# Folding a head's two output parts on TensorE with a constant 73x37 matrix, and dividing straight from PSUM

## What is computed

```python
qkv = h @ W_qkv + b_qkv
qkv = qkv.reshape(b, l, 3, H, D)
q, k, v = (qkv[:, :, 0], qkv[:, :, 1], qkv[:, :, 2])
scale = D ** (-0.5)
scores = jnp.einsum('blhd,bmhd->bhlm', q * scale, k)
attn = jax.nn.softmax(scores, axis=-1)
o = jnp.einsum('bhlm,bmhd->blhd', attn, v).reshape(b, l, c)
return o @ W_proj + b_proj
```

## Time and profile before

| | |
|---|---|
| median of 3 runs | 2692.27 us (2688.56 to 2693.1) |
| the profiled execution's own time | 2695.13 us |
| its span, first to last instruction | 2693.5 us |
| attention stage, about | 130 to 1500 us |
| TensorE busy (matmul records) | 2381.8 us, 88% |
| TensorE weight loads | 2048.1 us, 76% |
| VectorE busy | 1433.2 us, 53% |
| ScalarE busy | 1097.7 us, 41% |
| GpSimd busy | 772.7 us, 29% |
| mean granted TensorE clock | 0.939 |

### The profile page before, as it was taken

The page is one execution under the profiler, slowest core; times in us unless marked ns, Lnnn a source line. Parts: engine busy times, 40 slices in busy tenths (PEclk is TensorE's granted clock), DMA queues, the critical chain, the costliest instruction groups (busy, mean ns, idle before and its releaser), DMA issues. The chain is left out here.

```text
span 2693.5 us, 48930 instructions
## 1 busy us (share of the span) xinstructions
PE 2381.8 (88%) x15081; PEld 2048.1 (76%) x15081; DVE 1433.2 (53%) x2978; ACT 1097.7 (41%) x2362; POOL 772.7 (29%) x1547
## 2 busy tenths in 40 slices
PE   5698988988989789798998467999999999999998
PEld 1465766756767567576675457999999999999998
DVE  3577676676776766767766473333333333333332
ACT  1265555555555555555655122222222222222221
POOL 1043343343444344334445481111111111111110
PEclk9799989989989899898998688999999999999998
DMA  7122122231222222212221141010101010110100
GB/s 224 43 75 78 54 80 66 63 96 43 86 72 58 76 67 68 89 54 74 75 66 55 62 122 50 27 43 27 39 27 39 27 38 28 38 36 30 36 25 27
DMA packets 90196, 160.52 MB, mean 60 GB/s; under 512 B 22832, under 2 KB 34176, under 8 KB 89920
## 3 DMA queue, kind: packets, MB, share of 16 engines
q1 hardware_dynamic: 77056, 110.35, 14.2%
q0 software_dynamic: 11856, 46.60, 5.3%
q10 hardware_dynamic: 1024, 0.26, 0.0%
HBM read 80.10 MB, written 20.16 MB: 37 GB/s over the span
## 5 line engine op out<-in xcount | busy, mean ns | idle before, releaser
L1649 PE MATMUL bank<-h2T,w 128*128 128x256 f32 x4032 | 531.1, 283 | 9.3 <-issue 6.5
L1649 PEld LDWEIGHTS bank<-h2T,w 128*128 128x128 f32 x4032 | 508.0, 191 | 10.9 <-issue 7.6
L1558 DVE TENSOR_TENSOR glo<-bank,ghi 128x256 fp32r<-128x256 f32 x288 | 122.3, 425 | 688.2 <-ACT bank L1525 688.2
L1662 PE MATMUL bank<-w,ghi 128*128 128x288 f32 x2304 | 476.5, 298 | 0.4
L1524 ACT ACTIVATE ghi<-bank,b 128x256 fp32r<-128x256 f32 x288 | 137.1, 476 | 687.9 <-PE bank L1649 687.8
L869 DVE TENSOR_TENSOR plo<-pf,phi 128x512 fp32r<-128x512 f32 x512 | 365.3, 713 | 87.5 <-ACT pf L738 82.5
L735 ACT ACTIVATE phi<-bank 128x512 fp32r<-128x512 f32 x512 | 303.1, 592 | 252.0 <-PE bank L1049 226.5
L862 DVE TENSOR_REDUCE negm<-bank 128x1 f32<-128x512 f32 x512 | 349.5, 683 | 101.4 <-PE bank L1021 87.7
L1662 PEld LDWEIGHTS bank<-w,ghi 128*128 128x128 f32 x2304 | 367.2, 189 | 2.5 <-DVE x2T L1568 2.0
L1662 PE MATMUL bank<-w,glo 128*128 128x288 f32 x1152 | 340.8, 296 | 0.0
L738 ACT ACTIVATE pf<-bank 128x512 f32<-128x512 f32 x512 | 303.2, 592 | 0.0
(11 more groups left out here) (222 smaller groups left out, 3226.3 us busy)
## 6 DMA issues: line engine op xcount, KB each, us to landing
xln<-x POOLq DMA_DIRECT2D x16, 1152.0 KB, 6.8
qs<-qkhi SPq DMA_DIRECT2D x192, 72.0 KB
ks<-qkhi SPq DMA_DIRECT2D x192, 72.0 KB
wst<-w_fc POOLq DMA_DIRECT2D x34, 288.0 KB, 3.0
x_d<-xln POOLq DMA_DIRECT2D x32, 288.0 KB, 2.5
xa<-x_d SPq DMA_DIRECT2D x32, 288.0 KB, 2.8
xs<-x_d SPq DMA_DIRECT2D x16, 576.0 KB, 3.8
out<-xs SPq DMA_DIRECT2D x16, 576.0 KB, 2.9
```

What stands on the lines that cost most here:

```text
L1649: mm = pe.matmul(F[ft % 2][:, 0:CH], w1[0:rows, w, ft * PAR:(ft + 1) * PAR], h[0:rows, a, :], start=(i == 0), stop=(i == len(FULL_PASSES) ...
L1662: mm = pe.matmul(Y[2 * tt + half][:, 0:HALF], g[ft % 2][:, span], w2[:, ft, w, half * HALF:(half + 1) * HALF], start=(ft == 0 and i == 0), ...
```

## The change

TensorE no longer transposes `ots`. It multiplies it, as stationary operand, by a constant matrix `fold` of 73x37: the first 36 columns have a one at row j and one at row 37 + j, the last column a one at row 36. So the product is transposed and its parts are added in one step, and 37 columns a piece come out instead of 73. It is a plain fp32 product, as lines 997 and 1007 are. VectorE then takes the reciprocal, and multiplies from PSUM straight into `early` or `oo`; `oraw`, the reduction and GpSimd's `divide` go away. The semaphore `o_read` goes too: `o_norm` is raised by VectorE and takes its place in all waits. The two waits of `divide` (for `early_moved`, and for the last transposed output tile) move to VectorE. GpSimd gets a wait ahead of the second load of x, and `fold` is made by two VectorE instructions at the start of the stage.

```diff
-        oraw = [sb(acts, f"oraw{i}", [PAR, TT, HD]) for i in range(2)]
+        fold = sb(acts, "fold", [2 * HD + 1, HD + 1])
-        OW = 2 * HD + 2
+        OW = HD + 2
-        CONSTANTS = RING + 5
+        CONSTANTS = RING + 7
...
+                    if isinstance(b, int) and b == 1:
+                        pool.wait_ge(g_full, g_use(-1, ("ln", KT)) + 1)
                     load_x(pool, b)
...
-                def divide(b, n):
-
-                    h = (n // TT - 1) % HEADS
-                    pool.wait_ge(o_read, b * HEADS + n // TT + 1)
-                    if h < EARLY:
-                        if h == 0 and (not isinstance(b, int) or b >= 1):
-                            pool.wait_ge(early_moved, b)
-                        head = early[:, :, h * HD:(h + 1) * HD]
-                    else:
-                        if h == EARLY and (not isinstance(b, int) or b >= 1):
-                            pool.wait_ge(g_full, g_use(b, ("tr", TT - 1)) + 1)
-                        head = oo[:, :, h * HD:(h + 1) * HD]
-                    pool.tensor_tensor(head, oraw[h % 2][:, :, :], recip[h % 2][:, :].unsqueeze(2).to_broadcast([PAR, TT, HD]), ALU.mult).then_inc(o_norm, 1)
...
-                    if n % TT == 3 and is_there(b, n - TT):
-                        divide(b, n)
...
+                rows = ident[0:2 * HD + 1, :]
+                dve.tensor_tensor(fold[:, 0:HD], rows[:, 0:HD], rows[:, HD + 1:2 * HD + 1], ALU.add).then_inc(fixed, 1)
+                dve.tensor_copy(fold[:, HD:HD + 1], rows[:, HD:HD + 1]).then_inc(fixed, 1)
...
                     dve.wait_ge(oT, ho + 3)
-                    dve.wait_ge(o_norm, ho + 1)
                     dve.reciprocal(recip[i][:, :], view[:, :, HD]).then_inc(recip_done, 1)
-                    pair = view[:, :, 0:2 * (HD + 1)].rearrange("p t (two d) -> p t d two", two=2)[:, :, 0:HD, :]
+                    h = (n // TT - 1) % HEADS
+                    if h < EARLY:
+                        if h == 0 and (not isinstance(b, int) or b >= 1):
+                            dve.wait_ge(early_moved, b)
+                        head = early[:, :, h * HD:(h + 1) * HD]
+                    else:
+                        if h == EARLY and (not isinstance(b, int) or b >= 1):
+                            dve.wait_ge(g_full, g_use(b, ("tr", TT - 1)) + 1)
+                        head = oo[:, :, h * HD:(h + 1) * HD]
                     dve.wait_ge(recip_done, ho + 1)
-                    dve.tensor_reduce(oraw[i][:, :, :], pair, AX.X, ALU.add).then_inc(o_read, 1)
+                    dve.tensor_tensor(head, view[:, :, 0:HD], recip[i][:, :].unsqueeze(2).to_broadcast([PAR, TT, HD]), ALU.mult).then_inc(o_norm, 1)
...
                     pe.wait_ge(ot_done, ho + 2)
-                    pe.wait_ge(o_read, ho + 1)
+                    pe.wait_ge(o_norm, ho + 2)
...
                     for qt in range(TT):
-                        mm = pe.transpose(X[:, qt * OW:qt * OW + 2 * HD + 1], ots[i][:, qt * PAR:(qt + 1) * PAR],
-                                          ident[0:2 * HD + 1, 0:2 * HD + 1])
+                        mm = pe.matmul(X[:, qt * OW:qt * OW + HD + 1], ots[i][:, qt * PAR:(qt + 1) * PAR], fold[:, :], start=True, stop=True)
                     mm.then_inc(oT, 1)
```

More of the change, by code:

```diff
@@ L455, in build @@
         s_full, exp_f, exp_hi, p_lo, pv = sem("s_full"), sem("exp_f"), sem("exp_hi"), sem("p_lo"), sem("pv")
-        ot_done, oT, recip_done, o_read, o_norm = sem("ot_done"), sem("oT"), sem("recip_done"), sem("o_read"), sem("o_norm")
+        ot_done, oT, recip_done, o_norm = sem("ot_done"), sem("oT"), sem("recip_done"), sem("o_norm")
         early_moved = sem("early_moved")
@@ L553, in _ @@
                 pool.sem_inc(xo_done, 2)
-                pool.sem_inc(o_norm, 2)
                 pool.sem_inc(row_ready, 1)
@@ L799, in _ @@
                 dve.sem_inc(m_read, 2)
-                dve.sem_inc(o_read, 1)
+                dve.sem_inc(o_norm, 2)
                 def modulate(it, f):
@@ L964, in transpose_out @@
                         pe.wait_ge(early_moved, it)
-                    pe.wait_ge(o_read, it * HEADS + (TR_SLOT[qt] // TT + 1 if is_there(it, 0) else 1))
+                    pe.wait_ge(o_norm, it * HEADS + (TR_SLOT[qt] // TT + 2 if is_there(it, 0) else 2))
                     if is_there(it, TR_SLOT[qt] + 5):
@@ L1027, in transpose_max @@
                     if is_there(b, TT * (h - 3)):
-                        pe.wait_ge(o_read, b * HEADS + h - 1)
+                        pe.wait_ge(o_norm, b * HEADS + h)
                     pe.transpose(XM, negm[h % 2][:, :], ident[:, :]).then_inc(mT, 1)
```

## The result

The changed kernel takes 2734.64 us, median of 4 runs (2732.7 to 2737.6); the kernel before took 2692.68 us beside it. The ratio is 1.0155, 95% interval 1.0141 to 1.0169: slower by 42 us. The forecast was 2751, slower by 59 (than the 2692.3 that it started from).

The account below looks back on a forecast made before the run. TensorE's queue bounds the attention stage: 2695.1 + 88 (longer step) - 27 (covered by waits) - 1 (VectorE) - 1 (GpSimd) = 2754, forecast 2751 us since the profiled execution was 2.9 above the median; own range 2735 to 2770, outer 2715 to 2783.

Parts of the forecast that it names:

- What bounds the stage: Attention stage: most slots end when TensorE's queue ends; VectorE and ScalarE have slack and follow it.
- The price of a record: TensorE's new products: eight records a head at 0.111 us, 0.89 us against 0.31 for four transpositions, 0.58 extra.
- Rival 2: TensorE's products cost by the columns they move: at most 26 us extra, more than half covered, about 2702 us; chance 0.08.
- Half clock: Heads where TensorE runs at half clock: 19 of 128, each 1.31 us extra, 24.9 us in all.
- The cover: TensorE's later waits in the same slot, ten of 16 places, absorb 3.65 us an item, 27 us in all.
- My allowance for the first and last items: The first and last batch items cover less, so 3.65 us was multiplied by 7.3 items.
- the others: Slots outside the ten covering, three dense and three next to long gaps: -2 us forecast.
- VectorE, GpSimd: Relief from VectorE's shorter step and GpSimd's missing divide: 1 us credit each, ends 0 to 8 and 0 to 4.
- Rival 1: No cover: the waits behind TensorE's transposition move with it, 2780 us; chance 0.10.
- Rival 4: VectorE sets the slots, so TensorE's addition is free and VectorE's 0.17 us a head counts: 2671 us; chance 0.04.
- Rival 3: TensorE's clock falls less often with matmuls for transpositions; six full items lose 30 us, 2721 us; chance 0.08.
- Its own test: Signs in the trace: records 111 ns apart, step 1.12 us, items near 182 us, line 997's GpSimd waits smaller.

Follow-up runs that it names:

- the transposed kernel: Changed kernel with TensorE's four transpositions of 73 columns a head restored, VectorE still multiplying from PSUM, no GpSimd divide: 2690.44 us, ratio 0.9986 to the kernel before.
- eight heads in waiting slots: Changed kernel with the product only for eight heads an item where TensorE waits behind the step, the others transposed: 2696.05 us, ratio 1.0012 to the kernel before.
- the doubled products: Changed kernel with each of a head's four products issued twice, 16 records instead of 8: 2908.91 us, ratio 1.0811 to the kernel before.
- the filled kernel before: Kernel before with 40 idle transpositions of 128 columns in slot 40's wait for GpSimd, first seven items: 2682.41 us, ratio 0.9962.
- the filled changed kernel: Changed kernel with the same 40 idle transpositions of 128 columns in slot 40: 2724.31 us, ratio 1.0121 to the kernel before.
- plain products: Kernel before with 20 plain fp32 products of 64 moving columns, two records each, in slot 40's wait: 2698.27 us, ratio 1.002.
- the fp32r step: Changed kernel with ots and the matrix in fp32r, one record a product instead of two, 38 columns moving: 2717.55 us, ratio 1.0084 to the kernel before.

## Why the prediction was right, and where its size was off

**What bounds the stage.** Right. TensorE's queue was lengthened and the stage grew; the other engines were relieved and 1 to 6 us came of it (0.9986).

**The price of a record.** Right, and the step on which all rests. Line 1007's row said 0.110 us for 8 moving columns, the same as 128; the records stand 111 ns apart, the step takes 1.13 us from start to start (1.12 forecast), and with 73 or 128 columns it costs the same. Rival 2, that it goes by what it moves, is out. That the load is what costs was my reading of the row, and it is still not shown; the sum needs only the pitch.

**Half clock.** The term was mis-sized. I put 19 heads at 1.31 us. The count was right for the kernel before, by its granted clock; the head in slot 41 paid 1.13, since I took a pair of records of line 997 just behind a gap as typical. And I carried the share of before over: in slots 1 and 45 the step met full clock more often than I had it (at half clock in seven of these 16 heads, before in ten). The three slots took 17.5 us instead of 28.

**The cover.** The right places, too small: 27 us forecast, 46.4 - 9.6 = 37 measured in these slots. In the earlier trace rows I read the cover of slot 17 as the 0.32 in the brackets. Its neighbours, before:

```profile
856.84 0.33 PE L997 MATMUL bank<-chol,pick 128*128 128x64 f32 x2
857.49 1.20 PE L987 MATMUL bank<-wp,aT 128*128 128x288 f32 x7 [0.32 <-DVE qklo L827]
```

and after, with the wait gone:

```profile
877.97 0.33 PE L992 MATMUL bank<-chol,pick 128*128 128x64 f32 x2
878.11 1.17 PE L982 MATMUL bank<-wp,aT 128*128 128x288 f32 x7
```

The dense queue has 0.14 between these starts, the waiting one had 0.65. The slack was 0.51, not 0.32: the bracket counts from the modelled end of the record before, and in a dense queue the next instruction starts ahead of that. The slot grew by 0.08 (2.91 to 2.99), which is 0.59 - 0.51. I had the rule in the text, that only starts tell, and didn't hold to it here. Slots 21 and 61, which I also had from brackets (0.39), covered the whole step. In slots 9, 13, 25 and 29 a second piece was missed: the instruction behind the score product stood 0.34 behind it, in a dense queue 0.23 or 0.24, 0.1 us of slack more in each. Together that is 1.0 us an item, some 7 of the 10 us. The rest are slots that got shorter for other reasons, slot 33 by 0.35 in three items (in the transposed kernel too) and slot 9 by its clock in two. My allowance for the first and last items, 7.3 instead of 8, was about right: they covered 2.5 and 3.5 us, the six others 4.4 to 5.7.

In one place the mechanism was wrong: I had slot 49's wait for GpSimd as cover and nothing behind it. It covered its head's 4.6 us in its own slot, and slot 50 grew by 3.9. With that the cover is 33 us.

The two mis-sized terms, the cover by 10 us and half clock by 10.5, erred the same way, so neither hid the other; they are nearly the whole difference between 59 and the 37.8 of the traces. The 3.9 us of slot 50 were hidden: slots 0, 10 and 11 gave back 11.7 us through clock and waits that I hadn't forecast, and that the others came out near -2 was luck.

**VectorE, GpSimd.** Credit of 1 us each, measured 1 to 6 for both. The product is 17 ns longer than its estimate between the neighbours. The reciprocal, the moved waits and the new wait before the load of x cost nothing that shows: the reciprocal's wait for TensorE was 2.2 us and is 3.8 now, in one place.

**The rivals.** Rival 1, no cover, is out as a whole: eight heads in waiting slots pay 3 us. It seems to hold in one place, slot 49. Rival 4, VectorE sets the slots, is out by the transposed kernel. Rival 3 is half right. The clock was a second path of the change, but not in the direction of its page. The granted clock in whole items stayed at 0.91 to 0.94, and over the stage at 0.93; yet with the doubled products it fell to 0.89. The Trainium skill says in "TensorE: Matmul & The Clock Gate" (Part 4) that transpose mode does not count as busy for the clock in the same way. Here the traces disagree: in three items of the filled kernel before and in six of the filled changed kernel the clock rose from half to full while TensorE did nothing but transpositions, and in none of four items with plain products did it. By that rule the change should have gained clock; over the stage it stayed at 0.93.

**Its own test.** Items near 182 us were announced, 178.6 to 183.2 came; GpSimd's waits at line 997 were to shrink, and went from 50.5 us in 21 places to 44.2 in 10.

## What to carry to other kernels

A small matrix product in plain fp32 is two records here, and with 128 stationary columns they stand 111 ns apart whether 8, 37, 73 or 128 columns move; halving what comes out of it saves nothing, and a transposition of the same operand is cheaper (63 ns) though it moves twice as much. Work moved onto the engine that bounds a stage costs its length in the queue less the slack behind it in the same slot, and that slack is read from start to start against a dense slot, never from the idle time in the row. Look one slot further too: what a wait covers can come back as a longer wait behind it. Relief of an engine that is waited for in a few places was worth 1 to 6 us here, though some 75 us of work went away.

## What the runs showed of the hardware

- Two plain records of an fp32 product stand 111 to 112 ns apart at full clock and 213 at half, with 8 to 128 columns moving over 128 stationary ones; one fp32r record with 38 columns stands as far from the next. A transposition of 73 columns starts 63 ns behind the one before, one of 128 columns 109.
- Plain fp32 products without a gap don't always keep TensorE at 2.4 GHz: behind the doubled step 20 records took 2.87 us instead of 2.23 in slot 33, which ends at half clock in all eight items. Nor do they always bring it back: in four items with 40 records in the wait the clock was still at half when they ended, 8.24 us for what takes 4.58 at full clock.
- Transpositions with 128 moving columns brought it back: in all nine items in which it had fallen, of 14 with 40 of them in the wait, it was at full clock again before the 40 were through. That made the kernel before faster by 0.4%.
- Where the clock is gained in one place, part of it is lost in the next waits: 15.1 us saved in two slots, 11.1 given back in the two behind them.
- What sets the difference between products and transpositions, and why the fp32r step had the worse clock, wasn't settled; 128 moving columns instead of 37 gave 0.94 instead of 0.93, in the fastest run of four.
